# Six part and five value buffers in the first projections, block 0's first norms inside the last group of its causal attention, and a later turn of the first layer's tokens

## Time and profile before

| what | value |
|---|---|
| median of 3 runs | 1631.53 us |
| profiled execution, its own time | 1632.91 us |
| its span on the core | 1631.2 us |
| mean granted TensorE clock | 0.921 |
| TensorE matmul busy | 1360.8 us, 83% |
| VectorE busy | 1053.5 us, 65% |
| ScalarE busy | 753.9 us, 46% |
| GpSimd busy | 575.0 us, 35% |

### The profile page before, as it was taken

One profiled execution on the slowest core, in us unless ns is written; L12 is line 12 of the kernel. 1 busy time (PEld: TensorE's weight loads), 2 busy tenths in 40 slices (PEclk: granted clock), 3 DMA queues, 4 the chain that ended last, 5 costly groups with the idle time before them and its releaser, 6 DMA issues.

```text
span 1631.2 us, 21610 instructions
## 1 busy us (share of the span) xinstructions
PE 1360.8 (83%) x7242; PEld 778.2 (48%) x7242; DVE 1053.5 (65%) x2640; ACT 753.9 (46%) x1052; POOL 575.0 (35%) x456
## 2 busy tenths in 40 slices
PE   5778998998769978877999869799998678788896
PEld 3422333332258856543444336444443568544796
DVE  5777777777355357756566547665564778775754
ACT  5404555555667444542333535233335544254664
POOL 4001111111421033214776942068778437101212
PEclk8958999999979989997999979889999879799998
DMA  6853333330000000364213304634310020540001
GB/s 236 235 129 55 56 55 56 56 55 2 27 1 1 1 1 24 104 206 107 64 42 77 109 0 134 215 91 91 71 47 0 26 34 10 145 84 2 1 1 52
DMA packets 79848, 110.29 MB, mean 68 GB/s; under 512 B 16575, under 2 KB 55673, under 8 KB 77945
## 3 DMA queue, kind: packets, MB, share of 16 engines
q1 hardware_dynamic: 79737, 108.91, 26.8%
HBM read 70.55 MB, written 37.80 MB: 66 GB/s over the span
## 4 chain that ended last, share of the span: by engine, by line
PE 37%; DVE 20%; POOLq 20%; issue 10%; ACT 6%; DVEq 3%; DMA 2%; SPq 1%; POOL 1%; ACTq 0%
POOLq L1063 19%; PE banks L1162 5%; PE banks L1476 5%; PE banks L1461 4%; PE banks L2024 4%; PE banks L1104 4%; DVE max_parts L1299 3%; PE banks L1137 3%; DVE mask_rows L1295 2%; DVE scratch L1295 2%; PE banks L2050 1%; PE banks L1115 1%; PE banks L2007 1%; PE banks L2496 1%; PE banks L2040 1%
## 5 line engine op out<-in xcount | busy, mean ns | idle before, releaser
L1262 ACT ACTIVATE x_feat<-banks,key_bias 128x1024 f32<-128x1024 f32 x160 | 176.4, 1113 | 275.8 <-PE banks L1144 216.3
L1062 POOL TENSOR_TENSOR x_feat<-x_feat 128x1024 f32<-128x1024 f32 x112 | 269.1, 2402 | 80.4 <-ACT x_feat L1262 68.3
L1104 PE MATMUL banks<-stacks 128*128 128x512 f32 (+4 forms) x640 | 230.2, 408 | 35.2 <-DVE max_parts L1288 10.5
L1162 PE MATMUL banks<-x_feat,v_group 128*32 128x512 f32 (+4 forms) x1312 | 233.2, 571 | 8.1 <-ACT x_feat L1262 7.5
L1262 ACT ACTIVATE x_feat<-banks 128x1024 f32<-128x1024 f32 (+2 forms) x224 | 178.6, 840 | 122.4 <-PE banks L1137 120.6
L1104 PEld LDWEIGHTS banks<-stacks 96*128 96x128 bf16 (+1 forms) x640 | 77.1, 139 | 226.8 <-DVE max_parts L1288 88.3
L1074 POOL TENSOR_SCALAR_AFFINE_SELECT x_feat<-x_feat 128x256 f32<-128x256 f32 x128 | 52.0, 406 | 284.3 <-ACT x_feat L1262 283.0
L1137 PE MATMUL banks<-stacks 99*128 99x512 bf16 (+3 forms) x512 | 130.3, 344 | 21.1 <-ACT x_feat L1262 11.0
L1288 DVE CUSTOM_DVE_ANT_0 scratch<-banks,mask_rows 128x512 f32<-128x512 f32 x128 | 88.2, 689 | 57.7 <-PE banks L1104 57.6
L1143 PE MATMUL banks<-stacks 128*128 128x512 f32 x256 | 111.4, 435 | 9.5 <-DMA stacks<-neg_max_parts_r 9.5
L1461 PE MATMUL banks<-stacks 128*128 128x512 f32 x384 | 101.6, 403 | 8.2 <-DVE stacks L1443 4.0
(11 more groups left out here) (286 smaller groups left out, 2505.0 us busy)
## 6 DMA issues: line engine op xcount, KB each, us to landing
stacks<-q_parts_r SPq DMA_DIRECT2D x18, 512.0 KB, 12.0
stacks<-k_parts_r SPq DMA_DIRECT2D x18, 512.0 KB, 13.9
q_parts_r<-stacks SPq DMA_DIRECT2D x16, 512.0 KB, 3.1
k_parts_r<-stacks SPq DMA_DIRECT2D x16, 512.0 KB, 3.1
v_group<-v SPq DMA_DIRECT2D x14, 512.0 KB, 14.5
stacks<-q_parts SPq DMA_DIRECT2D x16, 384.0 KB, 5.0
w_even<-in_w SPq DMA_DIRECT2D x4, 1024.0 KB, 6.6
stacks<-q_parts SPq DMA_DIRECT2D x16, 256.0 KB, 5.4
```

The costliest lines, as they stand in the source:

```text
L1062: e.tensor_tensor(total, total, p, ALU.add)
L1104: m = e.matmul(PS[:, bank, at:at + wide], q[0:rows, h, qt * P:(qt + 1) * P], keys[0:rows, h, k0:k0 + wide], start=True, stop=True, skip_gr ...
L1162: m = e.matmul(PS[w * h:w * (h + 1), bank, t.q0:CH], V[:, h, :], PB[:, t.index % 2, h // 2, h % 2, 0:CH - t.q0], start=t.first, stop=t.las ...
L1262: e.activation(dst, PS[:, 2 * (st % 2):2 * (st % 2) + 2, 0:CH - t.q0], ACT.Exp, scale=A.scale, bias=bias).then_inc(s.p_ready, 1)
```

## The change

It has four parts.

1. **Projections.** The items go one feature, one value, in turn. There are six part buffers and five value buffers. ScalarE writes the first part from PSUM and, when VectorE has the remainder, the second part out of `RBUF`; VectorE makes the remainder directly from PSUM, and the third part one item later. VectorE's cast is gone.
2. **Last stores.** Stage 2 ends without a wait for its stores. In the attention SyncE waits for them before it loads group 1; VectorE waits for value buffers 3 and 4 (which are its scratch there) before the maxima of group 0, and for all of them at the start of group 0. The semaphores of the stores belong to stage 3.
3. **Norms of chunks 0 and 1.** `twice_vector` and `twice_scalar` run the sums, moments, roots, both gains and the second moments of these chunks inside the last attention group. The feed-forward stage begins with norm `nf`'s roots; the high part of the second half of the weights is copied by VectorE.
4. **First layer.** TensorE's and ScalarE's turn of the normalised tokens stands at the end of its step, and the forward product after `turn_weights`.

```diff
-    P3 = Y[:, 1024:4096].bitcast(BF16).rearrange("p (s k n) -> p s k n", s=4, k=3)
...
-    VT = [SCR[:, :], OT[:, :], VS[:, 1, P:P + CH], VS[:, 1, P + CH:P + 2 * CH]]
+    SPARE = WB[:, 2048 + P:2048 + P + 1536]
+    P3 = [x.bitcast(BF16).rearrange("p (k n) -> p k n", k=3) for x in
+          [Y[:, 1024 + 768 * i:1792 + 768 * i] for i in range(4)] + [SPARE[:, 768 * i:768 * (i + 1)] for i in range(2)]]
+    VT = [OT[:, :], VS[:, 1, P:P + CH], VS[:, 1, P + CH:P + 2 * CH]] + CAUSAL_SCR
+    RING, V_RING = len(P3), len(VT)
...
+            for it, v in zip(feat, vals):
                 yield True, it, nf
-                nf += 1
-            for v in vals:
                 yield False, v, nv
-                nv += 1
+                nf, nv = nf + 1, nv + 1
...
-                need(e, s.split, i - 3)
+                need(e, s.left, i - 3)
...
+        def second(it, i):
+            e.wait_ge(s.left, i + 1)
+            e.activation(part(it, i, 1), RBUF[:, i % 2, 0:it.n], ACT.Copy).then_inc(s.second_part, 1)
+        last = None
         for is_feature, it, i in in_order(sections):
             if not is_feature:
                 continue
             e.wait_ge(s.product, i + 1)
-            need(e, s.split, i - 1)
-            e.activation(RBUF[:, i % 2, 0:it.n], PS[:, i % 4, 0:it.n], it.func, bias=it.bias).then_inc(s.evacuated, 1)
-            if i >= 4:
-                e.wait_ge(s.stored[i % 4], 16 * (i // 4))
-            e.activation(part(parts, it, i, 0), PS[:, i % 4, 0:it.n], it.func, bias=it.bias).then_inc(s.first_part, 1)
+            if i >= RING:
+                e.wait_ge(part_stored[i % RING], 16 * (i // RING))
+            e.activation(part(it, i, 0), PS[:, i % 4, 0:it.n], it.func, bias=it.bias).then_inc(s.first_part, 1)
+            if last is not None:
+                second(*last)
+            last = it, i
+        second(*last)
...
+        def third(it, i):
+            e.wait_ge(s.second_part, i + 1)
+            e.tensor_tensor(part(it, i, 2), RBUF[:, i % 2, 0:it.n], part(it, i, 1), ALU.subtract).then_inc(s.split, 1)
+        last = None
         for is_feature, it, i in in_order(sections):
             if not is_feature:
                 value(it, i)
                 continue
             e.wait_ge(s.first_part, i + 1)
-            r = RBUF[:, i % 2, 0:it.n]
-            p1 = part(parts, it, i, 0)
-            if parts == 3:
-                p2, p3 = (part(parts, it, i, k) for k in (1, 2))
-                step(e.tensor_tensor(r, r, p1, ALU.subtract))
-                step(e.tensor_copy(p2, r))
-                e.tensor_tensor(p3, r, p2, ALU.subtract).then_inc(s.split, 1)
+            need(e, s.split, i - 1)
+            e.scalar_tensor_tensor(RBUF[:, i % 2, 0:it.n], PS[:, i % 4, 0:it.n], it.bias, part(it, i, 0),
+                                   ALU.add, ALU.subtract).then_inc(s.left, 1)
+            if last is not None:
+                third(*last)
+            last = it, i
+        third(*last)
...
-        stored_after(nf, nv)
...
+        if A is at0:
+            stored_after(e, *items0)
...
+    def twice_scalar(e, n2, idx):
+
+        if idx == 4:
+            for c in range(NC // B):
+                square_root(e, n2, c)
+        if 6 <= idx < 10:
+            normalise_pair(e, n2, (idx - 6) // 2, idx % 2, X, Y3)
+
+    def twice_vector(e, n2, nf, idx):
+
+        if idx in (1, 3):
+            e.drain()
+            attention_moments(e, n2, idx // 2)
+        if idx == 5:
+            for c in range(NC // B):
+                scaling(e, n2, c)
+        if idx in (9, 11):
+            c = idx // 2 - 4
+            e.wait_ge(n2.normed, 2 * c + 2)
+            e.tensor_tensor(four(Y3, c), four(Y3, c), wide(row(RA, ROWS_L0, "g2")), ALU.mult).then_inc(n2.weighted, 2)
+            second_moments(e, n2, c)
+            variance(e, nf, c)
...
+            if A is at0 and r == -1:
+                for u in (3, 4):
+                    e.wait_ge(value_stored[u], 16 * (items0[1] // V_RING))
             g = i * A.turn + r
+            if A is at0 and r == 0:
+                stored_after(e, *items0)
...
         split_high(e, sp, W0_FF, 0)
-        square_root(e, n2, 0)
-        for h in range(2):
-            normalise_pair(e, n2, 0, h, X, Y3)
-        split_high(e, sp, W0_FF, 1)
-        square_root(e, n2, 1)
-        context_keys_scalar(e, cs)
-        square_root(e, nf, 0)
+        for c in range(NC // B):
+            square_root(e, nf, c)
+        square_root(e, n2, 2)
         for h in range(2):
             normalise_pair(e, nf, 0, h, Y3, Y3)
-        normalise_pair(e, n2, 1, 0, X, Y3)
+        context_keys_scalar(e, cs)
+        context_values_scalar(e, cs)
         for k in range(KT):
             take_alone(e, tn, 0, k, 3, cols)
             split_tokens_scalar(e, s, tn, 0, k)
-        normalise_pair(e, n2, 1, 1, X, Y3)
-        context_values_scalar(e, cs)
-        square_root(e, n2, 2)
+        square_root(e, n2, 3)
...
-        attention_moments(0)
-        scaling(e, n2, 0)
-        attention_moments(1)
-        second_moments(0)
-        variance(e, nf, 0)
-        scaling(e, n2, 1)
-        scaling(e, nf, 0)
-        attention_moments(2)
-        add_row_to(e, 0, b2)
+    def attention_moments(e, n2, c):
+        e.tensor_tensor(four(X, c), four(X, c), four(Y3, c), ALU.add)
+        e.drain()
+        moments(e, c, X)
+        variance(e, n2, c)
+
+    def second_moments(e, n2, c):
+        bias_added(e, n2, c, Y3, row(RA, ROWS_L0, "be2"))
+        e.drain()
+        moments(e, c, Y3)
+
+    def first_ffn_vector(e, s, sp, zs, n2, nf):
+
+        b2 = row(RA, ROWS_L0, "b2")
+        attention_moments(e, n2, 2)
+        for c in range(NC // B):
+            scaling(e, nf, c)
+        e.wait_ge(sp.w_high, 1)
+        for i in range(4, 8):
+            a = slice(CH * i, CH * (i + 1))
+            h = e.tensor_copy(W_H[:, a], W0_FF[:, a])
+        h.then_inc(sp.w_high, 1)
+        scaling(e, n2, 2)
+        attention_moments(e, n2, 3)
         for k in range(KT):
             split_tokens_vector(e, s, 0, k)
-        second_moments(1)
-        attention_moments(3)
-        scaling(e, n2, 2)
+        scaling(e, n2, 3)
...
-            if i == 2 and ok(-1):
+            if i == 2 and not front and ok(-1):
                 e.wait_ge(nm.normed, c)
                 turn("y", c - 1, Y3)
-            if i == 3 and ok(-1):
+            if i == 3 and not front and ok(-1):
                 forward(c - 1, 0)
...
+            if i == 3 and front and ok(-1):
+                forward(c - 1, 0)
...
+            if i == 2 and front and ok(-1):
+                e.wait_ge(nm.normed, c)
+                turn("y", c - 1, Y3)
...
```

More of the change, by code:

```diff
@@ L93, in __init__ @@
     def __init__(self, s):
-        self.product, self.evacuated, self.split, self.step, self.v_product, self.v_taken, self.v_ready = s[0:7]
-        self.stored, self.v_stored, self.first_part = s[7:11], s[11:15], s[15]
+        self.product, self.left, self.split, self.second_part, self.v_product, self.v_taken, self.first_part = s
+class StoreSems:
+    def __init__(self, s):
+        self.parts, self.values = s[0:6], s[6:11]
 class AttentionSems:
@@ L604, in project_vector, with stored_after, project_sync @@
             e.wait_ge(s.first_part, i + 1)
[L605 to L622 removed]
+            need(e, s.split, i - 1)
[5 more added lines that the diff above has]
+        third(*last)
+    def stored_after(e, feat, val):
+        for u in range(RING):
+            need(e, part_stored[u], 16 * ((feat + RING - 1 - u) // RING))
+        for u in range(V_RING):
+            need(e, value_stored[u], 16 * ((val + V_RING - 1 - u) // V_RING))
+    def project_sync(e, s, sections, A):
         loads, feat, val = [], 0, 0
@@ L631, in load @@
             if pieces[k] == 0:
-                stored_after(*loads[k][2:])
+                stored_after(e, *loads[k][2:])
                 if k == 0:
@@ L654, in project_sync @@
                 load(k, LOAD_PIECES)
-        stored_after(nf, nv)
     def project(stage):
-        return sems(stage, ProjectSems, 16)
+        return sems(stage, ProjectSems, 7)
     def q_items(b, w, off, dst, bias, func, diag=False):
@@ L765, in attention @@
         A.halved = self_keys and dh == 64
-        A.norm = norm
+        A.norm, A.twice = norm, twice
         A.halves = [[i for i, (kind, h, of, _) in enumerate(A.chunks)
@@ L1265, in run @@
                     norm_scalar(e, A.norm, t.index)
+                if A.twice is not None and r == A.n - 1:
+                    twice_scalar(e, A.twice[0], t.index)
         each_step(A, e, run)
@@ L1406, in run @@
                     norm_vector(e, A.norm, idx)
+                if A.twice is not None and r == A.n - 1:
+                    twice_vector(e, *A.twice, idx)
         each_step(A, e, run)
@@ L1664, in first_ffn_gpsimd @@
         g2 = row(RA, ROWS_L0, "g2")
-        split_low(e, sp, W0_FF, 0)
-        for c in range(NC):
+        for half in range(2):
+            split_low(e, sp, W0_FF, half)
```

(17 more changed lines are left out.)

96 lines of the change are left out of this document (28 added, 68 removed).

## The result

The kernel after takes **1603.26 us** (median of 4, 1601.44 to 1607.62) against 1632.17 for the kernel before, measured beside it: ratio 0.9826, 95% interval 0.9802 to 0.985, or -28.9 us. The forecast was 1606, with a range from 1592 to 1621. A second measurement gave 1604.1 against 1632.98 (0.9818, 0.979 to 0.9847). The profiled span is 1601.8 us against 1631.2.

What follows compares the result with a forecast made beforehand. DMA was taken to bound sequence 1's projections, VectorE partly sequence 0's, norm chains the feed-forward front. Terms -9 + 9 - 10.6 - 5 - 10 = -25.6 took the profiled 1632.9 to 1607.3, median 1606; range 1592 to 1621.

Steps and rivals of the forecast that it cites:

- Projections, -9: Projections of sequence 0 and 1: VectorE's wait before group 0's maxima ends at 83 us, not 92; bounds -17 and -3.
- three more steps ... give 57 for value 9's store: Projections: after feature 10 at 54.1 us, three steps of 0.7 and SyncE's issue put value 9's store at 57.
- hidden tail: End of the projections: landings of stores behind value 14's, 1.97 MB, hidden by the attention's front, worth 6.2 us.
- barrier of value 17: Projections: value 17, five buffers behind value 12, sets a barrier shortly before the maxima; 1.4 us added.
- DMA is no bound: Rival, projections: mixed stores keep more requests open; -17 there, total -34, 1598 us; chance 0.12.
- Last group, +9: Last causal attention group: ScalarE's stop +4.4, four normalised pairs +2.4, lowered clock +2; bounds +4 and +15.
- The 3 us that I named: Last group: a stop of over 3 us lowers TensorE's clock, for which 2 us were added.
- Feed-forward front, -10.6: Feed-forward stage: first hidden product 15 us after the stage's start, not 25.6; bounds -5 and -13.
- Chunk 0, -5: Feed-forward chunk 0, first hidden product to turn: chunk 1's norm and a pair of table switches leave; bounds -2 and -8.
- First layer, -10: First layer: the turn behind ready work removes 12 of 15.5 us waited, part returns as VectorE's time; bounds -4 and -16.
- only changes places: Rival: the layer's turn gains only -2, the last group stretches by +15; total -11.6, 1620 us; chance 0.13.
- Slower by a lasting half clock: Rival: ScalarE's stop at tile 4 leaves TensorE at half clock; total about +23, 1655 us; chance 0.04.

Runs made afterwards that it cites:

- end_wait: The kernel after, with SyncE again waiting for all stores to land at the end of the projections; profiled span 1607.8 us, from one execution.
- scalar_values: The kernel after, with the stores of values 10 to 17 issued from ScalarE's queue instead of SyncE's; 1598.6 us (0.9779).
- Roots_later: The kernel after, with the last group's roots, VectorE's scales, normalised pairs and second moments one tile later; 1599.95 us (0.9797).
- layer_only: The kernel before with only part 4, the later turn in the first layer; 1622.62 us (0.9944).

## Why the prediction was right

The sum was -25.6; the stages give about -33 and the medians -28.9. Every term had the right sign and lay within its own bounds; no step failed, sizes did. That the total was met within 3 us is partly luck: the stages taken by themselves would have given about 1598, and single executions of the kernel before lie up to 10 us apart (1626.96 to 1636.63).

- **Projections, -9, measured -12.7.** The step that was mis-sized is "three more steps ... give 57 for value 9's store": it left at 54.5. I had let the context pairs end at 31 (29.5) and taken 2.67 us a pair (2.58). The load at 60 came at 57.7. From there to the maxima I had 23.0 us, and it was 22.4, but not by the terms that I had named: the hidden tail of 6.2 is 4.6 (end_wait), and the barrier of value 17, for which I added 1.4, isn't the last. Value 17 is written at 74.68, when value 12's store has landed, and SyncE is still issuing until 79.28. That these issues end the stage I hadn't foreseen (scalar_values); the two errors nearly cancel. The rival "DMA is no bound" falls by the landings.
- **Last group, +9, measured +8.2.** ScalarE's stop cost 4.7 against 4.4: exponentials at 407.0, where the old schedule would have had them at 402.3. What the four pairs cost no row separates; behind the longest wait leave seven gaps with 4.3 us, where I had read eight with 4.4. Under the half clock TensorE worked 5.9 us (408.1 to 414.0), so it cost at most 3 us where I had 2. The 3 us that I named are no limit: in the layer of after the granted clock was 0.5 from 601.8 us, behind a stop of 2.54 us. Roots_later shows that 3 of the 8.2 were avoidable.
- **Table loads.** The first load begins 0.02 us after the exponentials end (402.02), the root follows it within 0.01 us (402.04 + 1.28, root at 403.33), and the exponential likewise (405.73 + 1.28, 407.02). The drain of 1.38 us beside each load that the Trainium skill gives (ScalarE: Activation LUTs, "What ACT_TABLE_LOAD costs") doesn't show; without it the stop is 4.98 us, as measured.
- **Feed-forward front, -10.6, measured -9.4** (16.1 us against 15). VectorE's list was through at 13.6 us instead of 15, because only one of the four copies was held behind a subtraction of GpSimd (1.49 us, the others 0.41), where I had allowed for all four. The two splits took 2.35 instead of 1.5, because the second was held too. The 1.5 us that I took for a subtraction of GpSimd is a mean: in before they take 1.26, and one 2.32, beside VectorE's sum of 128x1024. The exclusive lock of the Trainium skill (SBUF — State Buffer, "SBUF: two separate sides") has both cases: there an operation of VectorE takes it in a two-port mode, or with two inputs in SBUF against a GpSimd operation that reads SBUF. I had told only the first. The traces agree: the copy and the splits end 0.28 and 0.55 us after GpSimd's subtraction, and the 128x4 operations within 0.02 us of it.
- **Chunk 0, -5, measured -6.1**, and 1.8 more in later chunks, which I had at nothing.
- **First layer, -10, measured -11.7.** The wait before the turn went from 15.5 to 0.5; the waits of the value products L2072 for VectorE stayed at 5.7 in all. New are 3.0 us of waiting for GpSimd (L2091) and 1.4 for VectorE (L2062), so little came back; the granted clock is 0.5 for 20.5 us of the layer instead of 30.7. The rival "only changes places" falls by layer_only.
- **Slower by a lasting half clock**: 6.8 us at half clock in the group, then full again until the next stage (431.1); it fell.

**Left open.** Both pairs of profiles put the two kernels 33 us apart at the layer's end, the medians 29 apart in all. Whether the rest takes some 4 us longer in most executions of after, or the profiled executions differ from the median ones, two profiles of each can't show. How the gain before the first load (6.0 us) divides between the new order, the missing casts and the rings is open as well.

## What to carry to other kernels

When transfers bound a stage, ask what waits for them and not only how many bytes there are: moving the wait for the last stores behind the next front gave 4.6 us, more than two additional part buffers and one value buffer (1.6). Before an operation is moved ahead on an engine, follow what it pushes back: an earlier hidden product was worth nothing because the root behind it came later. And a saving of a few us is to be read stage by stage, from the last mark that the edit can't have moved, and against a second profile of the same kernel: here the untouched half of the program moved by up to 12 us, and 1.7 of the 6.3 us of end_wait stood there before the edit acted. A mean over merged rows hides what happened: four copies in 2.50 us were three free ones and one that was held.

## What the runs showed of the hardware

- The issue of a store took SyncE 0.36 to 0.5 us at 52 to 60 us and up to 2.56 at 65 to 79 us, when the share of the DMA engines was 1.1; in the same stretch of scalar_values ScalarE's queue took one in 0.37.
- VectorE and GpSimd held each other for whole instructions. Beside a GpSimd subtraction of 128x512 (1.26 us by itself) a copy of 128x512 took 1.49 us instead of 0.41, a subtraction of 128x512 up to 1.74 instead of 0.68, and an operation on 128x4 1.06 to 1.21 instead of 0.16 to 0.24. Each ended within 0.02 us (128x4), 0.28 (copy) or 0.55 us (subtraction) of the end of GpSimd's. The other way round, a GpSimd subtraction took 2.33 us when VectorE's sum of 128x1024 (1.21) had begun 0.01 us before it. An operation that began when GpSimd's was nearly over lost little.
- Executions of the same projections began group 0's first load between 57.7 and 59.2 us, and took 22.2 to 22.6 us from it to the maxima.
